# A four-layer graph network on one core: who turns the running maxima of the last two softmax chunks

## The reference

```python
def _gat_layer(x, W, adj):
    proj = x @ W
    Wh, Ws = jnp.split(proj, 2, axis=-1)
    scores = Wh @ Ws.T
    a = jax.nn.softmax(scores, axis=-1) * adj
    out = a @ Wh
    out = out + x
    return jax.nn.leaky_relu(out, NEG_SLOPE)
x = inputs
for l in range(W_stack.shape[0]):      # two steps
    x = _gat_layer(x, W_stack[l], adj)
```

## Time and profile before

| | |
|---|---|
| median of 3 runs | 483.96 us |
| profiled execution | 483.51 us, of which the span of the trace is 481.7 us |
| TensorE matmul busy | 471.0 us (98%) |
| VectorE busy | 349.7 us (73%) |
| ScalarE, POOL busy | 235.8 us (49%), 187.4 us (39%) |

### The profile page before, as it was taken

One profiled execution on the slowest core, in us unless ns is written; L12 is line 12 of the kernel. 1 busy time (PEld: TensorE's weight loads), 2 busy tenths in 40 slices (PEclk: granted clock), 3 DMA queues, 4 the chain that ended last, 5 costly groups with the idle time before them and its releaser, 6 DMA issues. The chain is left out here.

```text
span 481.7 us, 5723 instructions
## 1 busy us (share of the span) xinstructions
PE 471.0 (98%) x1921; PEld 310.7 (64%) x1921; DVE 349.7 (73%) x760; ACT 235.8 (49%) x417; POOL 187.4 (39%) x186
## 2 busy tenths in 40 slices
PE   8999999999999999999999999999999999999994
PEld 7999755545555688887545444554556545778882
DVE  5688799999955799748133953992853399799994
ACT  5979379973887553323434531341333376342200
POOL 1444654552352068823000631461440064356641
PEclk9999999999999999999999999999999999999998
DMA  8955310000544000000000000000000000000001
GB/s 293 291 164 178 128 33 1 0 1 0 181 165 150 1 1 0 1 0 1 1 0 0 0 1 1 1 1 0 0 0 1 0 2 1 1 11 23 22 23 39
DMA packets 8180, 20.69 MB, mean 43 GB/s; under 512 B 1008, under 2 KB 4740, under 8 KB 8152
## 3 DMA queue, kind: packets, MB, share of 16 engines
q1 hardware_dynamic: 7144, 19.02, 11.9%
q0 software_dynamic: 464, 0.79, 0.7%
q10 hardware_dynamic: 544, 0.52, 0.3%
HBM read 18.94 MB, written 1.39 MB: 42 GB/s over the span
## 5 line engine op out<-in xcount | busy, mean ns | idle before, releaser
L1505 PE MATMUL psum<-QT,xT 128*128 128x512 f32 (+3 forms) x264 | 108.5, 542 | 0.0
L427 POOL TENSOR_TENSOR es<-es,ST 128x512 f32<-128x512 f32 (+3 forms) x60 | 75.1, 1252 | 51.2 <-ACT ST L627 49.4
L622 ACT ACTIVATE ST<-psum 128x512 f32<-128x512 f32 (+3 forms) x66 | 36.1, 547 | 86.8 <-DVE rm L985 77.6
L1505 PEld LDWEIGHTS psum<-QT,xT 128*128 128x128 f32 (+1 forms) x264 | 47.7, 186 | 40.4 <-issue 34.0
L985 DVE TENSOR_TENSOR rm<-psum,rm 128x512 f32<-128x512 f32 (+3 forms) x60 | 37.4, 624 | 38.7 <-PE psum L1505 38.4
L365 POOL TENSOR_TENSOR rstd<-veps,nhalf 128x1 f32<-128x1 f32 (+1 forms) x44 | 29.3, 667 | 68.9 <-DVE veps L769 68.9
L1619 PE MATMUL psum<-Wh,ST 128*128 128x256 f32 (+3 forms) x242 | 55.1, 380 | 0.0
L1549 PE MATMUL psum<-ST,Wh 128*128 128x512 f32 (+3 forms) x132 | 54.5, 542 | 0.0
L1317 PE MATMUL psum<-eb,x_all 128*128 128x512 f32 (+3 forms) x132 | 51.9, 542 | 0.0
L627 ACT ACTIVATE ST<-ST 128x512 f32<-128x512 f32 (+3 forms) x66 | 37.9, 579 | 28.4 <-DVE ST L1007 25.5
L393 POOL TENSOR_TENSOR esumb<-esumb,eb 128x1354 f32<-128x1354 f32 (+1 forms) x10 | 32.4, 3236 | 46.8 <-ACT eb L515 46.8
(11 more groups left out here) (173 smaller groups left out, 779.3 us busy)
## 6 DMA issues: line engine op xcount, KB each, us to landing
adj_rows<-in_adj_dram SPq DMA_DIRECT2D x10, 677.0 KB, 4.9
rows<-in_adj_dram SPq DMA_DIRECT2D x10, 677.0 KB, 4.0
x_all<-in_x_dram SPq DMA_DIRECT2D x5, 256.0 KB, 4.7
out_dram<-xs SPq DMA_DIRECT2D x10, 128.0 KB, 1.7
W<-in_L_gnn_W_stack_dram SPq DMA_DIRECT2D x2, 512.0 KB, 6.3
adj_rows<-in_adj_dram SPq DMA_DIRECT2D x1, 338.5 KB
rows<-in_adj_dram SPq DMA_DIRECT2D x1, 338.5 KB
w0n<-in_L_gnn_weight_dram SPq DMA_DIRECT2D x1, 256.0 KB, 2.8
```

What stands on the lines that cost most here:

```text
L427: nc.gpsimd.tensor_tensor(es[0:r, g % 2, 0:w], es[0:r, g % 2, 0:w], buf(g)[0:r, j, 0:w], ALU.add)\
L622: nc.scalar.activation(buf(g)[0:r, j, 0:w], psum[0:r, SB[n % 3], 0:w], ACT.Copy).then_inc(st_ready.sem, 1)
L1505: last = nc.tensor.matmul(psum[0:r, SB[n % 3], 0:w], xT[l][:, k, j * P:j * P + r], QT[:, k, c0:c1], start=(k == 0), stop=(k == KD - 1))
```

## The change

For chunks 4 and 5 alone, the maximum is made without TensorE. A new function `max_blocks(g)` on VectorE turns `rm` in blocks of 32 x 32 within each group of 32 partitions, reduces along the free dimension (`quad`), copies the four groups of 32 partitions side by side onto the first (`gathered`), reduces and negates again (`quadmax`), copies the result to the other three groups, and turns a broadcast of it into PSUM bank 7. `max_turn`, `max_reduce` and `max_spread` of chunks 4 and 5 are gone. `max_blocks(4)` stands where `max_reduce(4)` stood; `max_blocks(5)` stands after chunk 4's loop, ahead of `soft_step(5, 0)`, where `max_reduce(5)` stood inside that loop. Waits that the removed instructions made are moved to `den`.

```diff
+            def max_blocks(g):
+                w = chunk(g)[2]
+                nb = -(-w // BLOCK)          # BLOCK 32: nb is 16 for chunk 4, 11 for chunk 5
+                dve.wait_ge(rm_step.sem, T * (g + 1))
+                nc.vector.transpose(blocks[:, 0:nb * BLOCK], rm[:, g % 2, 0:nb * BLOCK]).then_inc(rm_blocked.sem, 1)
+                dve.wait_ge(rm_blocked.sem, g - SPREAD + 1)
+                own.link(nc.vector.tensor_reduce(quad[:, 0:nb], blocks[:, 0:nb * BLOCK].rearrange("p (b n) -> p b n", n=BLOCK), AX.X, ALU.max))
+                for a in range(QUADS):       # QUADS 4
+                    last = nc.vector.tensor_copy(gathered[:, a, 0:nb], quad[a * BLOCK:(a + 1) * BLOCK, 0:nb])
+                own.link(last)
+                own.link(nc.vector.tensor_reduce(quadmax[0:BLOCK, 0:nb], gathered[:, :, 0:nb].rearrange("p a b -> p b a"), AX.X, ALU.max,
+                                                 negate=True))
+                for a in range(1, QUADS):
+                    last = nc.vector.tensor_copy(quadmax[a * BLOCK:(a + 1) * BLOCK, 0:nb], quadmax[0:BLOCK, 0:nb])
+                own.link(last)
+                dve.wait_ge(sub_done.sem, T * g)
+                nc.vector.transpose(psum[:, 7, 0:nb * BLOCK], quadmax[:, 0:nb].unsqueeze(2).to_broadcast([P, nb, BLOCK]))\
+                    .then_inc(spread_ready.sem, 1)
 VectorE's order
-            max_reduce(4)
+            max_blocks(4)
             run_max(5, 0)
...
-                if s == T - 3:
-                    max_reduce(5)
...
+            max_blocks(5)
             for s in range(T + 2):
                 soft_step(5, s)
 den
-                pe.wait_ge(negmax_ready.sem, [2, 3, 3, 5, 6, 6][g])
+                pe.wait_ge(negmax_ready.sem, [2, 3, 3, 4, 4, 4][g])
+                if g == NC:
+                    pe.wait_ge(wh1_ready.sem, T)
 TensorE's order
             sum_n(0, 0, 2)
-            max_turn(4)
             s_tile(5, 0)
             sum_n(0, 2, 5)
-            max_spread(4)
             s_tile(5, 1)
...
-            sum_n(3, 0, 3)
-            max_turn(5)
-            sum_n(3, 3, 8)
-            max_spread(5)
-            sum_n(3, 8, T)
+            sum_n(3, 0, T)
             den(4)
```

More of the change, by code:

```diff
@@ L70, in gnn_stack @@
     TURNED = NC + 1
+    BLOCK = 32
+    QUADS = P // BLOCK
+    SPREAD = NC + 1
     NB3 = [2, 3, 5]
@@ L141, in gnn_stack @@
         idle = sb("idle", [P, 1])
+        blocks = sb("blocks", [P, BANK])
+        quad = sb("quad", [P, BANK // BLOCK])
+        gathered = sb("gathered", [BLOCK, QUADS, BANK // BLOCK])
+        quadmax = sb("quadmax", [P, BANK // BLOCK])
         negmax = sb("negmax", [P, EB])
@@ L257, in gnn_stack @@
         q_done, qT_ready, s_done, st_ready, rm_step = sem("q_done"), sem("qT_ready"), sem("s_done"), sem("st_ready"), sem("rm_step")
+        rm_blocked, spread_ready = sem("rm_blocked"), sem("spread_ready")
         max_turned, negmax_ready, max_ready = sem("max_turned"), sem("negmax_ready"), sem("max_ready")
@@ L1003, in soft_step @@
                     r = kk(j)
-                    if j == 0:
+                    if j == 0 and g < SPREAD:
                         dve.wait_ge(max_ready.sem, g + 1)
+                    elif j == 0:
+                        dve.wait_ge(spread_ready.sem, g - SPREAD + 1)
                     dve.wait_ge(st_ready.sem, g * T + j + 1)
@@ L1514, in max_turn @@
                     pe.wait_ge(NM.var_ready.sem, T)
-                if g == NC + 1:
-                    pe.wait_ge(wh1_ready.sem, T)
                 if g >= 2:
                     pe.wait_ge(rdb_ready.sem, 1 if g == 2 else NC)
-                if g == G - 1:
-                    pe.wait_ge(rden_ready.sem, NC + 1)
                 for n, i in enumerate(tiles(g)):
```

## The result

The changed kernel takes 485.66 us (median of 7 runs, 485.35 to 486.65), the kernel before 484.13 us (7 runs, 483.92 to 485.35). The ratio, which takes in all runs and not the medians alone, is 1.0026, with a 95% interval of 1.0014 to 1.0039: slower by 1.3 us, 0.7 to 1.9. The forecast was +0.6 us, 484.6, with 0.53 on a change too small to tell and 0.35 on slower by over 0.2%. The time lies inside the range; the measured 0.26% falls just on the side that had 0.35, and its interval takes in both. One profiled execution of each gives 483.51 and 485.48 us, 1.97 apart. Of these, 0.47 us lie ahead of the change: the last maximum of chunk 4's scores starts at 405.91 before and at 406.38 after, and nothing ahead of it differs between the two programs.

What follows compares the result with a forecast made beforehand. Bound by two nearly full engines, TensorE and VectorE, with TensorE's last product setting the end. -0.62 us at chunk 4 plus 3.27 at chunk 5 exceeds the 2.05 us slack by 0.60: 483.96 + 0.6 = 484.6 us, range 483.1 to 485.9.

Steps and rivals of the forecast that it cites:

- What bounds: From 416 us TensorE and VectorE both nearly full; TensorE needs chunk 5's last product with about 2.05 us slack.
- TensorE's gain, 1.85 us: Turns, spreads and a wait leave TensorE's queue: 0.88 us at chunk 4, 0.97 at chunk 5; the most to be gained.
- The block step, 3.80 and 3.27 us: VectorE's added turns, reductions and copies were to take 3.80 us at chunk 4 and 3.27 us at chunk 5.
- the floor: A block turn costs what a VectorE pass of its shape does: 0.69 us for 512 columns, 0.52 us for 352.
- the slow turn: Rival, chance 0.17: all four block turns run at half the pace of a pass, +2.4 us in all, 486.4 us.
- the linked price: Small copies in the block step counted as if linked, 0.18 us each plus 0.02: four copies 0.78 us, three 0.58.
- the cheap block step: Rival, chance 0.30: the small copies overlap, so chunk 5 costs 2.62 us and chunk 4 3.15; 482.3 to 483.7 us.
- Chunk 4, 0.62 us earlier: VectorE enters its saturated stretch 0.62 us earlier; chunk 4's first subtraction comes 0.2 us earlier, before 412.02.
- `max_reduce(5)`'s 0.53 us at nothing: Its removal from chunk 4's loop saves VectorE 0.53 us, counted as no gain since VectorE would meet the same POOL add.
- The displaced lock: Rival, chance 0.13: VectorE's stalls behind POOL's adds fall otherwise, one more of 0.4 to 1.0 us; 485.0 to 485.6 us.
- The sum: For the whole kernel: -0.62 + 3.27 = +2.65 us at chunk 5, more than the 2.05 us slack by 0.60 us.
- TensorE's waits: TensorE was to idle ahead of `den(4)` (0.4 us), `den(5)` (1.3 us) and output tile 8's last product.

Runs made afterwards that it cites:

- e4: The changed kernel with chunk 5's four copies, small reduction and three copies left out: last output tile read 1.50 us earlier than in the changed kernel.
- e12: The kernel before plus idle 32 x 11 copies ahead of chunk 5's first subtraction: four within one partition group took 0.38 us, four across groups 0.68 us.
- e1: Block step on VectorE for chunk 4 only, chunk 5 as in the kernel before: ratio to the kernel before 0.9994, last output tile read 0.53 us earlier.
- e2: Block step on VectorE for chunk 5 only, chunk 4 as in the kernel before: ratio to the kernel before 1.0041, last output tile read 2.04 us later.
- e7: The kernel before plus three idle 352-column block turns on VectorE ahead of chunk 5's first subtraction: last output tile read 0.58 us later.
- e8: The kernel before plus six idle 352-column block turns on VectorE ahead of chunk 5's first subtraction: last output tile read 2.27 us later.
- e11: The kernel before with only chunk 5's turns moved two products later in TensorE's order: ratio to the kernel before 0.9994 (0.9985 to 1.0004).

## Why the prediction was near, and short

- **What bounds.** Right: two full engines, with a slack between them that the change used up. Its size was off: 1.87 us, not 2.05. The working took the start of chunk 5's last piece of products from the chain, 463.64, and so 464.51 for the pass that needs the last product; TensorE's timeline has that piece start at 463.51 and end at 474.56 (shown above). Its last 46 passes took 10.20 us in the changed kernel, and 474.56 - 10.20 = 464.36, an estimate from these two rows, is 0.15 us sooner.
- **TensorE's gain, 1.85 us.** 1.69 by the timeline (the 26 passes took 5.79 us, not 5.63), all of it given back, as forecast. The last read, which TensorE's last product releases, is 1.49 us later all the same, so 1.69 + 1.49 = 3.18 us were lost to it from `den(4)` on. The three waits in brackets are 2.25 us of that; the other 0.93 us lie around the stops (4 passes in 1.11 us, for 0.87 at 0.217) and are not told apart further. They are not what sets the end: in e4, what VectorE's step is shortened by comes back in full.
- **The block step, 3.80 and 3.27 us.** 411.37 - 407.58 = 3.79 and 445.51 - 442.27 = 3.24. Turns at 0.70 and 0.53 us: the floor was right, the slow turn (0.17) is out. The copies at 0.69 and 0.68 for 0.78: near the linked price and not the 0.39 of overlap, so the cheap block step (0.30) is out; e12 shows why.
- **Chunk 4, 0.62 us earlier.** 416.29 - 406.38 = 9.91 against 416.42 - 405.91 = 10.51: 0.60. The mark that the forecast gave for it, chunk 4's first subtraction before 412.02, holds when counted from the anchor: 412.02 is 6.11 and it comes at 6.01 (at 412.39 on the trace's own clock). It is 0.1 and not 0.2 us earlier, as the two maxima ahead of it took 1.02 us, not 0.88.
- **`max_reduce(5)`'s 0.53 us at nothing.** Right: L1101 now starts earlier, takes 0.98, and L1102 ends where it ended, behind POOL (437.99 + 1.37 = 439.36, or 32.98 from the anchor, for 438.07 + 1.38 - 405.91 = 33.54: 0.56 earlier, which is chunk 4's shift alone).
- **The displaced lock.** Given 0.13 as a case of its own, priced at one stall of 0.4 to 1.0 us. It came, with 0.68 us. This is the step of the forecast that failed: "what is put ahead of it arrives in full", with both engines "shifted alike" behind it. The shift was alike, 0.36 and 0.35 us between the two, and yet the other engine was held: the first subtraction now stands behind a linked instruction. So an argument from equal distances could not rule the stall out.
- **The sum.** -0.60 + 3.24 and the links around it put the first subtraction 2.68 us later (forecast 2.65), the stall 0.68, the slack takes 1.87: +1.49 us in the trace, for +0.60 forecast. 0.68 of the missing 0.89 is the stall, 0.18 the slack. The time lies inside the range because the range reached over this rival (+1.0 to +1.6 us), not because +0.6 us was right.
- **TensorE's waits.** Foreseen at `den(4)` (0.69 for 0.4) and at the last product. The longest, 1.40 us for output tile 5's bank, was not: `sum_n(8)` needs the read of tile 5, which is VectorE's and as late as the rest. It is not what sets the end, for TensorE waits once more behind it, for the last product.

That the place of the step decides, and not its price as such, is shown by e1, e2, e7 and e8. Not shown is why POOL gets through first when the first subtraction stands behind a link: thirteen traces agree on when, none shows what decides between the two.

## What to carry to other kernels

Before work is moved to an engine that is nearly full, look for the place where that engine idles. The same 3.8 us of block turns gained 0.5 us where VectorE had waited for TensorE, and cost 2.0 where a whole chunk stood behind it. Slack is found by one subtraction in the table, and idle work of two lengths in the very place (e7, e8) confirms it and brings out the stalls that come along. And price small copies between groups of 32 partitions one by one, at their full length.

## What the runs showed of the hardware

- A block turn of 32 x 32 blocks in 32-bit floats costs about what VectorE's other 32-bit passes of that size cost here: 0.70 us for 128 x 512 (a reduction 0.69), 0.53 us for 128 x 352 (a reduction 0.52), and from a broadcast column into PSUM 0.73 and 0.56 us.
- Four copies of 32 x 11 take 0.38 us within one group of partitions, 0.68 us across groups, and 1.69 us beside one of POOL's adds.
- Where VectorE's two-input L1071 (L1101 after) overlaps POOL's add, one of them is held: 0.69 us on VectorE's (1.11 for 0.42, with POOL's at 1.18), or 0.64 us on POOL's (1.52 for 0.88). At the same distance between their starts, 0.35 us, e11 shows the one outcome and e12 the other.
